# A macaron layer on one core: softmax sums from a column of ones, two block turns on VectorE, and a new instruction order

## The reference

```python
x = x + 0.5 * ffn(layernorm(x), Wg, Wu, Wd)   # 8 experts, each silu(x @ wg) * (x @ wu) @ wd, 512 wide, all summed
x = x + attention(layernorm(x), w_q, w_k, w_v, w_o, rel_emb)
x = x + 0.5 * ffn(layernorm(x), Wg, Wu, Wd)

# attention: 16 heads of 8 dims, rotary q and k, causal, rel = rel_emb[clip(k - q, -32, 32) + 32]
scores = einsum('bhqd,bhkd->bhqk', q, k) + einsum('bhqd,qkd->bhqk', q, rel)
attn = softmax(where(causal, scores, NEG_INF))
ctx = einsum('bhqk,bhkd->bhqd', attn, v) + einsum('bhqk,qkd->bhqd', attn, rel)
```

## Time and profile before

| | us |
|---|---|
| median of 3 runs | 1380.24 |
| lowest and highest | 1378.69, 1386.11 |
| the profiled execution's own time | 1373.76 |
| its span, first to last instruction | 1371.8 |

### The profile page before, as it was taken

One profiled execution on the slowest core, in us unless ns is written; L12 is line 12 of the kernel. 1 busy time (PEld: TensorE's weight loads), 2 busy tenths in 40 slices (PEclk: granted clock), 3 DMA queues, 4 the chain that ended last, 5 costly groups with the idle time before them and its releaser, 6 DMA issues. The chain is left out here.

```text
span 1371.8 us, 29322 instructions
## 1 busy us (share of the span) xinstructions
PE 1333.0 (97%) x8472; PEld 1074.1 (78%) x8472; DVE 1192.4 (87%) x2554; ACT 1105.2 (81%) x2642; POOL 1098.6 (80%) x1012
## 2 busy tenths in 40 slices
PE   8999999999999999999999999999999899999798
PEld 7878777777878788778878878777888788788586
DVE  6887988998999999889899989899989889999465
ACT  6765878888888889878888888888888788888354
POOL 7977879788888888877779877889888788878465
PEclk9999999999999999999999999999999999999899
DMA  5404799999999999999999999999999989998200
GB/s 184 158 1 136 137 226 173 183 215 161 196 200 179 182 182 188 208 160 181 172 190 207 180 178 170 178 215 183 175 184 172 204 165 179 177 182 147 45 1 8
DMA packets 719138, 225.07 MB, mean 164 GB/s; under 512 B 653057, under 2 KB 698497, under 8 KB 718977
## 3 DMA queue, kind: packets, MB, share of 16 engines
q1 hardware_dynamic: 562224, 180.84, 73.4%
q10 hardware_dynamic: 156752, 42.36, 17.0%
HBM read 60.95 MB, written 69.86 MB: 95 GB/s over the span
## 5 line engine op out<-in xcount | busy, mean ns | idle before, releaser
L1231 POOL TENSOR_TENSOR hid_lo<-hid,hid_hi 128x512 fp32r<-128x512 f32 x512 | 662.1, 1302 | 149.2 <-ACT hid_hi L932 116.4
L1079 DVE TENSOR_TENSOR hid<-hid,work 128x512 f32<-128x512 f32 x512 | 347.1, 680 | 63.1 <-PE work L729 59.2
L1073 DVE SCALAR_TENSOR_TENSOR hid<-hid,work 128x512 f32<-128x512 f32 x512 | 345.2, 679 | 32.0 <-ACT hid L926 31.0
L1246 POOL TENSOR_TENSOR probs<-exps,probs 128x512 f16<-128x512 f32 (+1 forms) x288 | 307.2, 1069 | 79.0 <-ACT probs L989 76.0
L932 ACT CAST hid_hi<-hid 128x512 fp32r<-128x512 f32 x512 | 318.1, 625 | 62.0 <-DVE hid L1079 46.3
L926 ACT ACTIVATE hid<-work 128x512 f32<-128x512 f32 x512 | 307.1, 602 | 73.1 <-PE work L729 52.7
L977 ACT ACTIVATE exps<-work,negmax_shifted 128x512 f32<-128x512 f32 (+2 forms) x320 | 193.0, 605 | 40.9 <-DVE negmax_shifted L1179 25.4
L1173 DVE TENSOR_REDUCE negmax<-work 128x1 f32<-128x384 f32 (+3 forms) x352 | 222.2, 633 | 1.8
L727 PE MATMUL work<-xt,wg 128*128 128x512 f32 x512 | 205.3, 401 | 3.4 <-DVE xt L1048 1.5
L810 PE MATMUL acc<-hid_lo,wd 128*128 128x512 f32 x512 | 205.8, 405 | 0.8 <-POOL hid_lo L1231 0.7
L727 PE MATMUL work<-xt,wu 128*128 128x512 f32 x512 | 204.2, 399 | 1.0 <-DVE hid L1073 0.4
(11 more groups left out here) (99 smaller groups left out, 1909.2 us busy)
## 6 DMA issues: line engine op xcount, KB each, us to landing
prob_window_scratch<-probs SPq DMA_DIRECT2D x384, 80.0 KB, 3.0
rel_win<-rel_window_scratch ACTq DMA_DIRECT2D x250, 96.0 KB, 3.5
q_scratch<-rope SPq DMA_DIRECT2D x16, 512.0 KB, 4.7
qq<-q_scratch ACTq DMA_DIRECT2D x32, 256.0 KB
k_scratch<-rope SPq DMA_DIRECT2D x16, 512.0 KB, 3.9
rel_window_scratch<-g_s SPq DMA_DIRECT2D x32, 256.0 KB, 3.0
k_pad<-k_scratch SPq DMA_DIRECT2D x128, 64.0 KB, 3.1
prob_window_scratch<-probs SPq DMA_DIRECT2D x32, 256.0 KB, 4.8
```

What stands on the lines that cost most here:

```text
L1073: dve.scalar_tensor_tensor(out=hid[:, arg % HB, :], in0=hid[:, arg % HB, :], scalar=1.0, in1=work[bank_of["gate", arg]][:, :], op0=ALU.add ...
L1079: dve.tensor_tensor(hid[:, arg % HB, :], hid[:, arg % HB, :], work[bank_of["up", arg]][:, :], ALU.mult).then_inc(s_hid, 1)
L1231: pool.tensor_tensor(hid_lo[:, arg % HH, :], hid[:, arg % HB, :], hid_hi[:, arg % HH, :].bitcast(F32), ALU.subtract).then_inc(s_hlo, 1)
L1246: pool.tensor_tensor(probs[:, arg % PB, cols:2 * cols], exp_of(arg)[:, 0:cols], probs[:, arg % PB, 0:cols], ALU.subtract).then_inc(s_plent, 1)
```

## The change

1. `values` gets a column of ones, so that row 24 of each 32-row block of `ctx_p` holds the softmax sums (24 weight columns become 25). The number of matmuls stays the same. `accum_out` of exp goes away.
2. `recip_wide`, `recip_turned` and `recip_copy` go away. In their place DVE turns `ctx_p` in blocks of 32x32 into `ctx_s` (`denominators`), takes the inverses of 16 columns of that (`recip`), and turns them, each read 32 times, back into `ctx_s` (`spread`). `band_values` waits for the first turn, since it writes to the bank that is read. `denominators` waits for the second stage of `values` and for the last group's `outproj`.
3. q and k lie on the partitions in the order of the dims, with the four heads side by side: `load_q` becomes one pattern of 128 rows, and the four DMAs of `load_k` write every fourth partition.
4. The first `gate` of a pass waits only for the high part of its input, makes two matmuls and then waits for the low part.
5. The 24 transposes of the identity become 14.
6. `UNITS_TO` becomes 1394, the planned cost of exp falls, `project_v` is wished 8 units later, and all of `LATER` is new. So the list is in a different order throughout.

```diff
+    VD = VS * DH + 2
-    UNITS_FROM, UNITS_TO = 146, 1406
+    UNITS_FROM, UNITS_TO = 146, 1394
-    LATER = {"acc": -121.4, "attention_sum": -318.4, "band_turn": -1036.1, "band_values": -446.9, "constants":
...
+    LATER = {"acc": -1001.3, "attention_sum": -224.3, "band_turn": -664.1, "band_values": -890.3, "constants":
...
-        step("PE", 0.683, at, "gate", n, ("gated", back(n, 2)), split[0], *normed)
+        step("PE", 0.683, at, "gate", n, ("gated", back(n, 2)), split[0], *normed, ordered=rest)
-        step("PE", 1.33, end + 24, "project_v", t, ("ln_lo", ("ln2", t)), ("qk_store", (t, 1)))
+        step("PE", 1.33, end + 32, "project_v", t, ("ln_lo", ("ln2", t)))
-            step("PE", 0.47, at, "band_values", gg, ("band_turn", gg), ("values", VG * gg))
-            step("DVE", 0.1, at - 8, "recip", gg, ("exp", GK * (gg + 1) - 1), ("recip_wide", back(gg, 2)))
-            step("POOL", 1.0, at - 7, "recip_wide", gg, ("recip", gg), ("outproj", back(gg, 1)))
-            step("PE", 0.44, at - 4, "recip_turned", gg, ("recip_wide", gg))
-            step("ACT", act_wide(L), at - 4, "recip_copy", gg, ("recip_turned", gg), ("outproj", back(gg, 1)))
+            step("PE", 0.47, at, "band_values", gg, ("band_turn", gg), ("denominators", gg))
+            step("DVE", wide(L) + 0.06, at, "denominators", gg, ("values", VG * gg + VG - 1), ("outproj", back(gg, 1)))
+            step("DVE", 0.2, at, "recip", gg, ("denominators", gg))
+            step("DVE", wide(L) + 0.06, at, "spread", gg, ("recip", gg))
...
-        values = sb("values", [P, 2, NT, HQ, HG, VS, DH], BF16)
+        values = sb("values", [P, 2, NT, HQ, HG, VD], BF16)
...
-                        sp.dma_start(k_pad[R * a:R * (a + 1), arg % 2, a, :].bitcast(F32),
+                        sp.dma_start(k_pad[a:P:HQ, arg % 2, a, :].bitcast(F32),
...
-            for i in range(24):
+            for i in range(14):
                 done = pe.transpose(work[0][:, 0:P], ident[:, :], ident[:, :])
...
-                        pe.wait_ge(s_xlo, LN["ln1" if kind == "A" else "ln3", t] + 1)
-                    bank = take_bank(name, arg)
-                    three(bank[:, :], wg[:, HI, e, cols], wg[:, LO, e, cols],
-                          x_hi, x_lo).then_inc(s_gate, 1)
+                    bank = take_bank(name, arg)
+                    pe.matmul(bank[:, :], wg[:, HI, e, cols], x_hi, start=True, stop=False)
+                    pe.matmul(bank[:, :], wg[:, LO, e, cols], x_hi, start=False, stop=False)
+                    if k == 0:
+                        pe.wait_ge(s_xlo, LN["ln1" if kind == "A" else "ln3", t] + 1)
+                    pe.matmul(bank[:, :], wg[:, HI, e, cols], x_lo, start=False, stop=True).then_inc(s_gate, 1)
...
-                        act.activation(exp_of(arg)[:, n * keys:(n + 1) * keys], scores[:, n * keys:(n + 1) * keys], ACT.Exp,
-                                       scale=-1.0, bias=bias,
-                                       accum_out=denom[:, gg % 2, i, a:a + 1]).then_inc(s_exp, 1)
+                                       scale=-1.0, bias=bias).then_inc(s_exp, 1)
...
                 act.dma_start(qq[:, arg % 2, :].bitcast(F32),
                                  bass.AP(q_t, t % VB * 4 * P * L + g * L,
-                                         [[HG * L, HQ], [H * L, 4 * DH], [1, L]])).then_inc(s_qld[arg % 2], 16)
+                                         [[HG * L, P], [1, L]])).then_inc(s_qld[arg % 2], 16)
...
+                if name == "denominators":
+                    dve.wait_ge(s_pv, VG * (arg + 1))
+                    wait(dve, s_o, arg)
+                    dve.transpose(ctx_s[:, :], ctx_p[:, :]).then_inc(s_den, 1)
                 if name == "recip":
-                    dve.wait_ge(s_exp, NQ * (arg + 1))
-                    dve.reciprocal(rdenom[:, arg % 2, :, :], denom[:, arg % 2, :, :]).then_inc(s_rc, 1)
+                    dve.wait_ge(s_den, arg + 1)
+                    dve.reciprocal(rdenom[:, :], ctx_s[:, VS * DH:L:R]).then_inc(s_rc, 1)
+                if name == "spread":
+                    dve.wait_ge(s_rc, arg + 1)
+                    dve.transpose(ctx_s[:, :], rdenom[:, :, None].to_broadcast([P, L // R, R])
+                                  ).then_inc(s_spread, 1)
```

More of the change, by code:

```diff
@@ L119, in step @@
-    def step(engine, takes, time, name, arg, *after, lands=None):
-        before = ()
+    LATER = {"acc": -1001.3, "attention_sum": -224.3, "band_turn": -664.1, "band_values": -890.3, "constants":
+             1133.0, "denominators": 54.7, "down": 35.1, "down_lo": 29.5, "exp": -173.7, "fill": 412.2, "gate": 23.6,
+             "gated": 71.3, "hi": -198.0, "largest": -162.3, "ln_hi": -529.1, "ln_lo": -689.7, "ln_rstd": 1093.6,
+             "ln_scaled": 32.2, "ln_stats": -1470.7, "ln_turned": -124.5, "lo": -374.9, "load_band": -993.3, "load_expert":
+             -463.4, "load_k": 142.9, "load_q": -750.4, "load_window": 12.7, "load_x": -324.4, "near": -107.3, "outproj":
+             -284.8, "p_hi": -363.4, "p_lent": -428.7, "p_lo": -1802.0, "p_turn": 164.5, "prepare_hi": -319.7,
+             "prepare_lo": -35.4, "product": -41.0, "project": -175.8, "project_v": 67.5, "qk_hi": -1126.2, "qk_lo":
+             -852.9, "qk_store": -488.3, "qrel": 45.9, "qrel_copy": -281.8, "qrel_store": -903.5, "recip": -701.6,
+             "rotate": 1052.3, "scale": -1319.7, "scores": 8.4, "shift": -711.3, "split_hi": 141.7, "split_lo": -128.0,
+             "spread": -416.4, "store": 545.7, "store_band": -200.3, "sum": 625.1, "sum_turned": -565.4, "tanh": -333.1,
+             "up": 26.1, "v_add": 325.1, "v_split": 205.7, "values": -488.4, "zero": 1202.6}
@@ L121, in step @@
+    def step(engine, takes, time, name, arg, *after, lands=None, ordered=()):
+        before = []
         if name in ("p_lo", "p_lent", "shift"):
@@ L127, in step @@
         steps[name, arg] = (engine, takes, LANDS[engine] if lands is None else lands, time + LATER.get(name, 0.0),
-                            [what for what in after if what[1] is not None], [what for what in before if what in steps])
+                            [what for what in after if what[1] is not None],
+                            [what for what in before if what in steps] + list(ordered))
     PARTS = {"split_hi": 3, "split_lo": 3, "project": 4, "rotate": 4, "qk_hi": 2, "qk_lo": 2, "qk_store": 2}
@@ L223, in macaron_kernel @@
             step("DVE", wide(L) + w % 2 * 0.9, at, "rotate", (t, w), ("project", (t, w)))
[L224 to L225 removed]
+        step("PE", 1.33, end + 32, "project_v", t, ("ln_lo", ("ln2", t)))
+        step("DVE", wide(L), end + 32, "v_add", t, ("project_v", t), ("qk_store", (t, 1)))
         for i in range(SPLITS):
@@ L281, in macaron_kernel @@
                 step("DVE", 0.07 * HEADS[i], due[k] + 0.8, "shift", k, ("largest", k))
-            step("ACT", HEADS[i] * 0.235 + columns / 1200, due[k] + 1, "exp", k, ("shift" if lent(k) else "largest", k),
+            step("ACT", HEADS[i] * 0.07 + columns / 1200, due[k] + 1, "exp", k, ("shift" if lent(k) else "largest", k),
                  ("p_lent", lent_before(k, EB) if lent(k) else None))
@@ L303, in macaron_kernel @@
     BANKS = 6
-    TAKES = {"gate": ("bank", "gated"), "up": ("bank", "product"), "scores": ("bank", "done_with"), "qrel": ("bank", "qrel_copy"), "recip_turned": ("bank", "recip_copy"),
+    TAKES = {"gate": ("bank", "gated"), "up": ("bank", "product"), "scores": ("bank", "done_with"), "qrel": ("bank", "qrel_copy"),
              "outproj": ("bank", "attention_sum"), "sum_turned": ("bank", "sum"), "ln_turned": ("bank", "ln_lo"),
@@ L885, in _ @@
                     done.then_inc(s_bv, 1)
-                if name == "recip_turned":
-                    bank = take_bank(name, arg)
-                    pe.wait_ge(s_rw, arg + 1)
-                    transposes(bank, ctx_s).then_inc(s_rdt, 1)
                 if name == "outproj":
@@ L1055, in _ @@
             dve.memset(zeros[:, :], 0.0)
+            dve.memset(values[:, :, :, :, :, VS * DH:VS * DH + 1], 1.0)
             dve.memset(eps[:, :], EPS).then_inc(s_half, 1)
-            dve.memset(carried[:, :, :], 1.0 / SCALE).then_inc(s_carried, 1)
-            dve.wait_ge(s_carried, 1)
-            for k in range(GK):
-                g, i, a = TASKS[k]
-                if lent(k):
-                    done = dve.memset(carried[:, i, a:a + HEADS[i]], 1.0)
-            done.then_inc(s_carried, 1)
             dve.wait_ge(s_x[0], 16)
```

62 lines of the change are left out of this document (16 added, 46 removed).

## The result

| | before | after |
|---|---|---|
| median of 4 runs | 1379.47 | 1342.53 |
| lowest and highest | 1377.18, 1386.11 | 1341.76, 1343.26 |
| the profiled execution's own time | 1373.76 | 1341.76 |
| its span | 1371.8 | 1340.0 |
| PE busy, idle in the span | 1333.0, 38.8 | 1314.1, 25.9 |

What follows compares the result with a forecast made beforehand. PE was taken as the bound, busy 97% of the span. The terms, -14.1 + 5 + 0.9 - 4.5 - 3 - 0.8 - 0.7 = -17.2, gave an own time of 1356.6 and a median of 1363 us, range 1351 to 1377.

Steps and rivals of the forecast that it cites:

- What bounds the kernel: Whole span: PE is the bound, busy for 97% of it, so what comes off PE comes off the time.
- The loads of q and k: DMA loads of q and k: same bytes in the same number of DMAs, so 0.
- The turned probabilities: Waits of `values` for the DMA that turns probabilities: five waits shorten by 0.9 us each, -4.5, ends -16 to +5.
- the rival in which the waits vanish: All five DMA waits of `values` and the slow-clock stretches go: 11 us more gain, 1352; chance 13%.
- ACT's relief: Accumulator reads (64.7 + 41.5 us) and 19.1 us of copies leave ACT; claimed worth 0 by itself.
- The transposes: Four transposes of the inverses leave PE in each of 32 groups, 0.44 us a group: -14.1 us.
- the term's +5: Attention beside feed-forward: 64 turns of 0.60 us bring DVE to 96%; cost +5 us, ends 0 and +20.
- The estimate of 1.24 us a turn: DVE's block turns: four skill-page transposes of 311 ns per turn would make the DVE cost about +22, the gain gone.
- The 25th column: One weight column more in the matmuls of `values`: between 0 and 1.7 us, taken as +0.9.
- Banks: PE's other 8.2 us of idle, where banks are reused with little work between: -3, ends -8 and +2.
- The start: Kernel start with ten fewer idle transposes: gain 1.5 us, less a possibly later clock rise; taken as -0.8.
- The first gate of the last pass: Start of the last pass: first two matmuls run while DVE makes the low part, -0.7 us.

## Why the prediction was right in sign and wrong in size

**What bounds the kernel** was right: PE, busy for 97% of the span before and 98% after.

**The loads of q and k: this step failed.** The prediction says "the same bytes in the same number of DMAs: 0, with their ends inside those of the DMA term". Bytes and number were the wrong measure. The number of engines changed from 4 to 16, and the new load was worth 26 us in the kernel before and 44 us in the kernel after. The row that could have told it was shown. The load on ACT's queue 2.3 us before it was left unread, and I called the long issue congestion, "which no edit touches".

**The turned probabilities** were costed at -4.5, from a distance of 73 matmuls instead of 69. The mechanism was wrong. With the new distance and the old load the waits grew to 15.6 us; with the old distance and the new load they shrank to 1.1. The bound of -16, "all five waits and three slow-clock stretches", was short of what the new load took away in the kernel before: 12.4 us of idle time and 8.8 us of busy time, 21 us by the spans. I had given the rival in which the waits vanish 13%, and ascribed it to ACT's relief and the distance. The waits did vanish, but by the load of q, and the time went 10 us below that rival's 1352. That its time was nearer than my forecast's is luck.

**The transposes:** -14.1 forecast; four transposes a group put back cost 12 to 17.

**DVE:** the turns have 0.70 us and DVE stands at 96% as forecast, and 1.4 us of waiting ahead of the first turns is little. Whether the term's +5 was right can't be told alone. Its reasoning was too easy: 40 us more of turns cost 30 us, so the "44 us of slack" were mostly not there to be used. The estimate of 1.24 us a turn, worked out from the Trainium skill's page "VectorE: DVE Perf Modes", section "The three transpose paths", is refuted by the measured 0.70.

**ACT's relief** was put at 0 by itself, and its accumulators alone cost 9 us or more when they are put back. "Neither ends PE's waits often" was true of the rows. That a longer chain from scores to probabilities delays what stands behind it is argued, not shown; this too may depend on the order, which was made for the shorter chain. The relief was also smaller than the 64.7 + 41.5 us that I read as leaving ACT: 40.0 us of busy time.

**The 25th column:** 0, not +0.9. The stage of 48 matmuls has 0.85 us as in the earlier trace rows and is followed 0.78 us after its start as there, and that of 32 0.56 us after as before. This was the lower end, by which the 128 moving columns set the time.

**Banks:** PE's idle time from 150 to 1250 us other than for `probs_t` went from 8.2 to 7.3 us, so -0.9 where I had -3.

**The start:** the sign was wrong. The twelfth matmul starts at 15.12 us and started at 14.01, so +1.1 where I had -0.8. I had seen the danger (the gap of 1.4 us was forecast, and measured 1.39) but allowed for seven slow matmuls; there were eleven (7 to 14 in the nine traces). The Trainium skill's rule, page "TensorE: Matmul & The Clock Gate", section "Part 4: PE-mode transpose", that transposes don't count as busy in the same way would leave the number of idle transposes without effect on the clock. The two starts above differ by ten transposes alone, and by which level the first gate gets; and in three traces the clock rose behind 14 transposes and nothing else. The traces speak against it.

**The first gate of the last pass** starts 0.02 us after DVE begins the low part, where it started 0.79 after it:

```profile
1266.86 0.69 DVE L1035 TENSOR_TENSOR xt<-work,xt 128x512 fp32r<-128x512 f32 x1 [5.23 <-ACT xt L947]
1266.88 0.80 PE L784 MATMUL work<-xt,wg 128*128 128x512 f32 x1 [0.68 <-ACT xt L947]
```

-0.77, as forecast.

**The sum.** Without the rows of q and k my terms sum to -17.2; the kernel with everything but them came out 8 us slower than before. So the sum would have been wrong in sign without the part that it valued at nothing. It can't be said that the other parts are worth +8 as such: in the presence of the fast load they are worth -10 to -12 (1352.1 to 1342.5; by the ratios 12), against the -17.2 of the sum. It may be that late probabilities cost more where DVE is fuller, since a DVE that stands ahead of a turn stands with PE. It may as well be that the new table was made for the fast load. No run tells the two apart.

What stays open: how the difference of 18 us between the two prices of the load (26 and 44) divides between DVE's load and the table; and whether keeping PE's clock up across the 5.5 us wait ahead of the last pass, still there in both kernels, would gain anything. It wasn't tried.

## What to carry to other kernels

Cost a DMA by the engines that it can use, not by its bytes alone: the pattern whose outermost dimension has 4 entries held 4 of 16 engines for 3.8 us in place of 1.9 on all, and transposes issued behind it on the other queue came late. When an issue on one queue is long, read the other queue's last rows before calling it congestion. And in this kernel a planner's table of wished times belonged to one set of steps: undo edits with the table left in place, say that the price so found is one in that order, and don't read a table's worth from an exchange.

## What the runs showed of the hardware

- With a load of 256 KB on four DMA engines, DMA transposes on the other queue took up to 6.56 us to issue (median 1.25), fifteen of them 3.5 us or more. On sixteen there was one such issue, and the kernel took 26 us of 1378 less, at the same bytes.
- A block turn of 128x512 in f32, from PSUM and also from a source read 32 times over, takes 0.70 to 0.71 us on DVE, about the same as a multiplication of that size (0.68).
- A 25th weight column under 128 moving columns costs nothing that can be seen: 48 matmuls in a row take 0.78 us with 24 and with 25 (median of 32 groups each).
- An accumulator read by exp has 0.20 to 0.23 us, but 512 of them (110.8 us) add only 40.0 us to ACT's busy time.
- 96 more DMA issues on ACT's queue, 46 us of its time, cost this kernel 30 us, about as much as 40 us of work more on DVE (30 us).
- 14 transposes and a gap of 1.39 us left PE at 1.2 GHz for the next four transposes and eleven matmuls (7 to 14 matmuls in nine traces); 24 transposes with a gap of 0.20 us left it at 2.4 GHz, as in all five traces with 24.
